# The residual loads of the output projections issued by SyncE instead of GpSimd

## What is computed

```python
x = x + attn_a(layernorm(x), ...)     # causal attention, 16 heads of 64
x = x + ffn(layernorm(x), ...)        # full attention whose projections are W x + gated low-rank experts
x = x + attn_b(layernorm(x), ...)     # retention scan, layer norm, silu gate
x = x + ffn(layernorm(x), ...)
```

## Time and profile before

| What | us |
|---|---|
| median of 2 runs | 4269.77 |
| lowest and highest | 4269.24, 4270.3 |
| the profiled execution | 4264.47 |
| its span on the slowest core (core 1) | 4262.9 |
| spans of the 8 cores | 4246.0 to 4262.9 |

### The profile page before, as it was taken

One profiled execution on the slowest core, in us unless ns is written; L12 is line 12 of the kernel. 1 busy time (PEld: TensorE's weight loads), 2 busy tenths in 40 slices (PEclk: granted clock), 3 DMA queues, 4 the chain that ended last, 5 costly groups with the idle time before them and its releaser, 6 DMA issues. The chain is left out here.

```text
span 4262.9 us, 40907 instructions; the slowest of 8 cores (4246.0 to 4262.9 us)
## 1 busy us (share of the span) xinstructions
PE 3112.2 (73%) x13815; PEld 1273.6 (30%) x13815; DVE 1318.5 (31%) x1955; ACT 1612.7 (38%) x1600; POOL 126.2 (3%) x162
## 2 busy tenths in 40 slices
PE   2677788876447888888887566375377888888875
PEld 0223333334123233333334122132132333333242
DVE  4333333334352211111115256521622111111141
ACT  2034444451200566666660300123003666666710
POOL 0000000000000000000000000010000000000000
PEclk6788788879668888888888777687588888888898
DMA  2201000002321000000002422034211000000014
GB/s 90 30 5 11 6 6 6 1 13 70 96 40 20 8 7 5 6 5 3 1 1 60 119 20 20 0 57 141 30 24 11 6 6 6 6 6 1 1 38 141
DMA packets 138717, 119.22 MB, mean 28 GB/s; under 512 B 119801, under 2 KB 128138, under 8 KB 129180
## 3 DMA queue, kind: packets, MB, share of 16 engines
q0 software_dynamic: 128480, 71.31, 10.2%
q1 hardware_dynamic: 10044, 45.31, 3.4%
HBM read 120.81 MB, written 33.55 MB: 36 GB/s over the span
## 5 line engine op out<-in xcount | busy, mean ns | idle before, releaser
L794 ACT ACTIVATE ringf<-psd,negcb 128x1024 bf16<-128x1024 f32 x1024 | 1059.9, 1125 | 601.2 <-PE psd L742 600.5
L794 ACT ACTIVATE ringa<-psd,negcb 128x1024 bf16<-128x1024 f32 x320 | 337.3, 1117 | 363.2 <-PE psd L742 332.2
L722 PE MATMUL psb<-ringf,vprf 128*65 128x512 bf16 x1024 | 445.2, 435 | 10.4 <-ACT ringf L794 9.1
L739 PE MATMUL psd<-qpairf,kpairf 64*128 64x512 bf16 x1024 | 422.2, 425 | 28.3 <-ACT ringf L794 5.6
L742 PE MATMUL psd<-qpairf,kpairf 64*128 64x512 bf16 x1024 | 430.4, 432 | 0.0
L726 PE MATMUL psb<-ringf,vprf 128*65 128x512 bf16 x1024 | 423.2, 413 | 0.0
L696 PE MATMUL psb<-c_IDENT,densf 1*128 1x1 f32 x1024 | 167.4, 289 | 172.7 <-DVE act L896 172.7
L739 PEld LDWEIGHTS psd<-qpairf,kpairf 64*128 64x128 bf16 x1024 | 91.8, 95 | 458.6 <-issue 457.4
L696 PEld LDWEIGHTS psb<-c_IDENT,densf 1*128 1x128 f32 x1024 | 163.8, 246 | 190.2 <-issue 190.2
L1120 PE MATMUL psd<-act,wobf 128*128 128x512 bf16 x512 | 141.1, 426 | 89.4 <-DVE xnf L1151 87.3
L722 PEld LDWEIGHTS psb<-ringf,vprf 128*65 128x65 bf16 x1024 | 114.1, 111 | 301.9 <-issue 294.2
(11 more groups left out here) (276 smaller groups left out, 4091.7 us busy)
## 6 DMA issues: line engine op xcount, KB each, us to landing
xof<-Xs POOLq DMA_DIRECT2D x16, 1024.0 KB, 9.0
lnsta<-xT SPq DMA_DIRECT2D x8, 1024.0 KB, 6.6
xoa<-xT POOLq DMA_DIRECT2D x8, 1024.0 KB, 9.4
Xs<-xna SPq DMA_DIRECT2D x8, 1024.0 KB, 5.3
Xs<-xnf SPq DMA_DIRECT2D x8, 1024.0 KB, 5.3
xob<-Xs POOLq DMA_DIRECT2D x8, 1024.0 KB, 9.1
Xs<-xnb SPq DMA_DIRECT2D x8, 1024.0 KB, 5.3
y<-xnf SPq DMA_DIRECT2D x8, 1024.0 KB, 5.3
```

The source lines that it names most:

```text
L722: t.matmul(PSB[4][0:65, :], VP[tkpv][:, hA * 65:hA * 65 + 65], RING[slot][:, 0:512], start=(tkpv == 0), stop=(tkpv == n - 1))
L739: t.matmul(pd[:, 0:512], KP[p % 2][0:64, ks], QP[p % 2][0:64, cs], start=True, stop=True, tile_position=(0, 0))
L794: ex.inc(s.activation(RING[slot][:], pd[:], AF.Exp, bias=NEGC[:, p:p + 1], scale=softmax_scale))
```

## The change

The loads of the old residual leave GpSimd's stream and go into SyncE's, ahead of the store that waits for the same event. GpSimd's stream keeps the weight slices alone. All waits on buffers stay what they were: load k after VectorE's tile k-2, slice j after TensorE's tile j-2. All four stages are changed alike, since they come from one function.

```diff
             off = NC if ffn else 0
-            wob_dma(0)
-            wob_dma(1)
-            for dt2 in range(ND):
-                if dt2 >= 2:
-                    g.wait_ge(vo.sem, vo0 + nxvso_holder[0] + NC * (dt2 - 1))
-                oq[dt2 % 2].inc(
-                    g.dma_start(XOLD[dt2 % 2][:],
-                                src_res[dt2 * 128:(dt2 + 1) * 128, :]), 16)
-                j = dt2 + 2
-                if j < ND:
+            for j in range(ND):
+                if j >= 2:
                     g.wait_ge(to.sem, to0 + off + (j - 1) * NC)
-                    wob_dma(j)
+                wob_dma(j)
...
             for dt2 in range(ND):
-                _store(sync, dt2)
+                if dt2 >= 2:
+                    sync.wait_ge(vo.sem, vo0 + nxvso_holder[0] +
+                                 NC * (dt2 - 1))
+                oq[dt2 % 2].inc(
+                    sync.dma_start(XOLD[dt2 % 2][:],
+                                   src_res[dt2 * 128:(dt2 + 1) * 128, :]), 16)
+                if dt2 >= 2:
+                    _store(sync, dt2 - 2)
+            _store(sync, ND - 2)
+            _store(sync, ND - 1)
```

## The result

| What | us |
|---|---|
| before, median of 10 runs beside it | 4271.3 |
| changed kernel, median of 12 runs | 4141.9 |
| its profiled execution, also its lowest time | 4131.6 |
| its span on the slowest core (core 3) | 4130.1 |
| spans of its 8 cores | 4108.0 to 4130.1 |

The ratio is 0.9675, with a 95% interval of 0.9655 to 0.9695: the change makes the kernel faster by 3.25%, about 139 us. It leaves out executions in which the cores of a die ran at a lower clock, which the median of all 12 contains. The forecast was 4070. The kernel is faster, as forecast with 0.93, but the time lies outside the range of 4034 to 4113.

The account below looks back on a forecast made before the run. Late-issued residual loads were taken to bound the four output projections. Gains of 49.9 (a1), 47.5 (f1), 49.9 (f2) and 48.6 (b1), together 195.9 us off 4264.5, gave 4068.6; predicted 4070, range 4034 to 4113.

Parts of the forecast that it names:

- rival of issue time: Output projections: moving the load saves only the slice's 0.87 us issue in 24 of 32 tiles, 21 us, 4243; chance 0.05.
- The load with its store isn't the bound: Output projection tiles: load and store starting together allow a tile of 7.6 us, not the bound but near it.
- S: Time until load k and store k-2, started together when tile k-2 is done, have both landed; about 9.9 us.
- The slice is late next: Weight slice, issued when TensorE ends tile k-2, becomes late; TensorE waits 1 to 3 us at every second tile.
- Lw: Weight slice's time from issue to landing, taken as 9.9 us; 7.4 beside one 1 MB store today.
- the whole bundle: A tile's three transfers, load, store and weight slice: 8.8 us of DMA engine work and 1.1 to start and signal.
- My own upper bound: Weight slice's landing: if one megabyte ahead costs 3.4 us and there are now two, 10.8 us.
- packet rule: Each DMA engine takes turns between its queues packet by packet, so the small-packet slice would land last.
- After shorter waits I take 0.5 each: TensorE's slower clock after slice waits of 2 to 3 us: 0.5 us each, 1.5 in all for a1's three.
- The slice lands in time: Output projections: TensorE sets the pace, stages of 61.9 to 68.7 us, gains together 228, time 4036; chance 0.21.
- DMA-bound: Output projections: a third megabyte ahead makes the slice land after 13.3 us, 41 us more in all, 4110; chance 0.21.
- Slower: Slices starve beside SyncE's two megabytes per tile; as slow as now at 26.3 us, 4305 at 29.7; chance 0.02.

Follow-up runs that it names:

- run 2: Kernel before with only the order changed, slice j first, then load j, both on GpSimd; ratio to before 0.9508, lowest 4066.8 us.
- run 3: Kernel before with all slices issued at the stage's start and loads on GpSimd behind them, waiting for VectorE alone; ratio to before 0.9478, lowest 4054.2 us.
- run 1: Changed kernel with all eight weight slices issued at the stage's start, each with its own counter; ratio to before 0.9482, lowest 4054.8 us.
- run 11: Run 4 with the next load, its double and the next store held until the slice before has landed; lowest 4178.6 us.
- run 5: Changed kernel with load 3, and store 1 behind it, held until slice 2 has landed; ratio to before 0.9682, lowest 4132.0 us.
- run 8: Run 1 with the store ahead of the load on SyncE and b1's first load held until slice 0 landed; ratio to before 0.9494, lowest 4050.7 us.
- run 6: Changed kernel with every load from 3 on held until the slice before has landed; ratio to before 0.9674, lowest 4127.2 us.
- run 4: Changed kernel with every load from the third on issued twice, second time into a spare buffer; ratio to before 0.9995, lowest 4266.9 us.

## Why the prediction was right, and where it was wrong

**What bounds the kernel: right.** The load's late issue was the bound, and it stood behind a slice that waited for TensorE. Runs 2 and 3 remove that order without SyncE, and gain more than the change does. That also answers the rival of issue time (4243), which is out: the changed kernel is 111 below it. The Trainium skill, "DMA: Bandwidth & Descriptors", section "Issuing engines are not separate DMA queues", says that transfers of several engines share the same 16 DMA engines. That agrees with run 3, which leaves the loads on GpSimd and is as fast as run 1. Its second half, that spreading issues saves only issue time, misses what the trace shows here: an issuing engine's stream is in order, and a wait in it holds back everything behind, as the load of the earlier trace rows, which starts only at 4199.39, right behind the slice's issue.

**The load with its store isn't the bound: right.** S was forecast at 9.9; the store lands after 9.2 to 9.9, the load after 7.2. No addition waits for `xo`.

**The slice is late next: right, but its Lw was too small.** The mechanism held; what failed is the price of a wait in the sum, and Lw is its first term: "I take Lw = 9.9, the same as for the whole bundle". It measured 11.2 to 12 in most cases on all cores (in the middle 11.6). My own upper bound, 3.4 us per megabyte beside the slice, gave 10.8 and was the better one, and even it was short. The series in the runs is 4.0 alone, 7.4 beside one megabyte, 11.5 beside two, 15.5 beside three (run 11): some 4 each, added to the slice's own 4.0. The 9.9 took the bundle's 8.8 us of work for the whole delay. That work was measured where the load ran behind the slice in one queue, with only the store beside it. By the packet rule that the prediction takes from the Trainium skill, "DMA: Bandwidth & Descriptors", section "Queues, rings and completion order", the slice would land last, and the trace agrees: it mostly lands 0.9 us after its store (slice 2 of f2 on core 1 at 4047.6, the store at 4046.8).

**The waits were priced too low.** A wait, with what follows, was Lw + 0.5 ("After shorter waits I take 0.5 each"). It is Lw + 0.7 for the way from the tile's end to GpSimd's issue, which I had left out, and 1.9 for the clock: the three tiles behind a wait in f2 of core 1 take 9.46, 9.37 and 10.27 us (the last from 4091.64 to 4101.91), not some 7.8. My upper bound for this, 2.2, was nearly it. I had set it aside because I expected waits of 2 to 3 us; at 4 to 5 they are as long as the one in the earlier trace rows.

**Two terms weren't in the sum.** A slice that hasn't landed when the next tile's two megabytes start can be caught by them: 17.5 us on core 3 in a1, 18.0 in b1. With these held back (run 5) the same slices took 13.6 and 12.0. And b1's first matmul comes 8.8 us after GpSimd's issue, not 5.6, and its first 64 matmuls then take 15.3, not 13.8, behind an idle time of 11.5.

The account for core 3, with Lw and clock from the rows of core 1: 12 waits at 1.6 (Lw 11.5), 0.7 and 1.4 (clock) more than forecast are 44; two caught slices at 6 are 12; b1's start 3.2 and 1.5 are 5. Together 61 of the 63.3 that are missing. (One of the 12, before tile 6 of f1, is put down to ScalarE's cast in the view: cast and slice ended within 0.1 us.) So Lw alone is 19 of the 63, and with 11.5 in its place the forecast would have been some 4089, inside the range; the issue (8), the clock (17) and the caught slices (12) took the time out of it. The last of these is arithmetic on one core: run 5, in which no slice 2 was caught in a1 or b1, was no faster.

**The rivals.** "The slice lands in time" (4036) is what runs 1, 3 and 8 made true: 4051 to 4055, with b1's start and some late transfers on top. "DMA-bound", 4110, came nearest to the time, but its mechanism, a third megabyte ahead of each slice, is seen only for the caught slices; holding the next load off (runs 5 and 6) brought nothing. The share of the DMA engines is 0.91 in a tile without a wait and 0.67 in one behind a wait, and runs 1, 3 and 8 move the same bytes through the four stages in some 70 to 77 us less, so the engines aren't the limit over a stage. "Slower" asked for Lw of 26.3, with six megabytes beside the slice, to be as slow as before. Run 4 has slices of mostly 21 to 27 us, three megabytes of their own tile and three of the next beside them, and a time within 0.3% of before. Point and price were placed well; what the argument missed is that a third megabyte per tile is enough to bring in the next tile's.

What stays open: why an equal slice is caught on some cores and not on others. The next load starts 7.2 to 11.2 us after every slice 2, 4 or 6 of the changed kernel, while all of them are in flight, and only 5 of the 96 took 17.5 or more; none lies between 13.7 and 17.5.

## What to carry to other kernels

Where a load is late, look first at what its issue stands behind. Moving a wait or an issue within the queue can be worth more than moving the load to another engine, and a buffer with room of its own for each piece (here the weight slices) needs no wait at all. When transfers are made to start together, price the smallest-packet one as its time alone plus a full share for each megabyte beside it (here some 4 us), and ask whether it still ends before the next round begins. Price a new TensorE wait with what comes behind it: here 0.7 us to the issue and 1.9 us of slower clock, on top of the 4 to 5 of the wait.

## What was not expected of the hardware

A 256 KB slice of 512-byte rows took 4.0 us alone and 7.4, 11.5 and 15.5 beside one, two and three megabytes of the other queue, nearly a straight line, and mostly 21 to 27 when the next three came before its end. A slice of twice the bytes in as many packets took 12.0 to 12.8 in half of the cases, where the single one took 11.6 in the middle. In the tiles behind waits of 4 to 5 us in f2 of core 1 the granted clock was 0.75 to 0.83, which costs a tile of 7.8 us 1.6 to 2.5 more; behind 16 idle matmuls in the wait, 32 matmuls took the 7.08 us of full pace.
